# Attention and a routed expert layer: chosen experts only, side work between attention slots, scores on 64 contraction rows

## The reference

```
mask = where(diff > 0, -inf, 0);  cond = abs(diff) <= 64
mask = maximum(maximum(mask, where(cond, 0, -inf)), -1e9)   # all keys up to 64 ahead, and every key behind
attn = softmax(q * HEAD_DIM**-0.5 @ k.T + mask);  x = layernorm(x + (attn @ v) @ out_w.T + out_b)

scores = sigmoid(x @ router.T); sc = scores + e_bias
tidx   = top 4 of the 16 experts, out of the 2 best of 4 groups of 4;  tw = scores[tidx] / sum * 2.5
routed = sum over the 4 chosen e of tw[e] * (silu(x @ gate[e].T) * (x @ up[e].T)) @ down[e].T
shared = (silu(x @ sh_gate.T) * (x @ sh_up.T)) @ sh_down.T      # 2 experts' width, every token
x = layernorm(x + routed + shared)
```

## Time and profile before

| | us |
|---|---|
| median of 3 runs (range) | 1291.25 (1289.18 to 1295.77) |
| span of the profiled execution | 1287.9 |
| PE, DVE, ACT, POOL busy in it | 1214.8, 947.5, 625.9, 238.9 |
| projection, until the first attention slot | 0 to 99.8 |
| 16 attention rounds | 99.8 to about 644, some 31 to 34 each |
| expert stage | about 647 to 1283 |

### The profile page before, as it was taken

How to read it: one execution, slowest core, us unless ns; L and a number is a source line. 1 busy time by engine, 2 the same in 40 slices (tenths; PEclk the granted TensorE clock), 3 DMA queues, 4 the chain that set the end, 5 groups by cost and what they waited for, 6 DMA issues and landing times.

```text
span 1287.9 us, 28066 instructions
## 1 busy us (share of the span) xinstructions
PE 1214.8 (94%) x8448; PEld 644.6 (50%) x8448; DVE 947.5 (74%) x1975; ACT 625.9 (49%) x1366; POOL 238.9 (19%) x432
## 2 busy tenths in 40 slices
PE   7877999999999999999799999898998989989997
PEld 4543444444444444443356666565665656556564
DVE  7587888888888888887657776676776767757754
ACT  4415777777777777777633332323222232222332
POOL 8831222222222222222401010010200102000000
PEclk9998999999999999999999999898999999999999
DMA  5631111111111111110131232121312212122220
GB/s 166 187 116 53 38 39 39 37 37 37 37 37 37 37 34 32 34 36 14 46 84 61 48 99 59 61 71 43 90 49 63 77 51 90 50 47 77 59 82 33
DMA packets 62443, 76.78 MB, mean 60 GB/s; under 512 B 8992, under 2 KB 37408, under 8 KB 62368
## 3 DMA queue, kind: packets, MB, share of 16 engines
q1 hardware_dynamic: 60736, 72.80, 19.2%
q10 hardware_dynamic: 1632, 3.15, 0.8%
HBM read 62.94 MB, written 12.85 MB: 59 GB/s over the span
## 4 chain that ended last, share of the span: by engine, by line
PE 64%; DVE 13%; issue 9%; ACT 7%; SPq 2%; POOL 2%; DMA 2%; DVEq 0%; ACTq 0%; POOLq 0%
PE bank L759 16%; PE bank L604 11%; PE bank L572 9%; PE bank L587 9%; PE bank L772 9%; DVE hf L1192 3%; DVE sg L1185 3%; ACT hh L947 3%; ACT a_PT L863 3%; PE bank L647 2%; PE bank L575 2%; PE bank L688 1%; PE bank L628 1%; PE bank L651 1%; SPq L324 1%
## 5 line engine op out<-in xcount | busy, mean ns | idle before, releaser
L984 DVE TENSOR_REDUCE a_mx<-bank 128x1 f32<-128x512 f32 (+3 forms) x720 | 401.2, 618 | 73.7 <-PE bank L575 44.6
L863 ACT ACTIVATE a_PT<-bank 128x512 f32<-128x512 f32 (+4 forms) x832 | 357.0, 505 | 138.1 <-PE bank L587 137.5
L587 PE MATMUL bank<-a_QS,a_KS 113*128 113x512 f16 (+4 forms) x832 | 269.6, 331 | 11.4 <-ACT a_PT L863 6.1
L572 PE MATMUL bank<-a_KS,a_QS 112*128 112x512 f16 (+4 forms) x832 | 258.6, 332 | 15.5 <-DVE a_mx L984 8.3
L947 ACT CAST hh<-hf 128x512 f16<-128x512 f32 x144 | 89.0, 618 | 332.5 <-DVE hf L1192 332.5
L509 POOL TENSOR_SCALAR_AFFINE_SELECT a_PT<-a_PT 128x256 f32<-128x256 f32 (+1 forms) x288 | 109.6, 381 | 419.0 <-ACT a_PT L863 418.7
L604 PE MATMUL bank<-a_PT,a_VG 128*17 128x512 f32 (+4 forms) x1664 | 179.7, 504 | 6.4 <-POOL a_PT L509 6.4
L772 PE MATMUL bank<-dh,hh 128*128 128x256 f16 x576 | 159.0, 276 | 16.9 <-DVE z L1207 16.9
L1199 DVE TENSOR_TENSOR hl<-hf,hh 128x512 f16<-128x512 f32 x144 | 99.8, 693 | 99.4 <-ACT hh L947 99.4
L772 PE MATMUL bank<-dh,hl 128*128 128x256 f16 x576 | 159.1, 276 | 0.0
L772 PE MATMUL bank<-dl,hh 128*128 128x256 f16 x576 | 159.1, 276 | 0.0
(11 more groups left out here) (134 smaller groups left out, 1438.2 us busy)
## 6 DMA issues: line engine op xcount, KB each, us to landing
cb<-c_dram SPq DMA_DIRECT2D x128, 256.0 KB, 3.3
q_dram<-p_qk SPq DMA_DIRECT2D x32, 128.0 KB, 2.1
k_dram<-p_qk SPq DMA_DIRECT2D x32, 128.0 KB, 2.1
a_QS<-q_dram SPq DMA_DIRECT2D x64, 64.0 KB
a_KS<-k_dram SPq DMA_DIRECT2D x64, 64.0 KB
xb<-x SPq DMA_DIRECT2D x8, 512.0 KB, 3.6
out<-oo SPq DMA_DIRECT2D x8, 512.0 KB, 4.2
p_xf<-xT ACTq DMA_DIRECT2D x6, 512.0 KB, 4.2
```

Source lines behind the costliest of these rows:

```text
L572: mm = pe.matmul(bank[:, at:at + hi - lo], QS[p][0:MR, t // NT, h, t % NT * P:t % NT * P + P], KS[p][0:MR, piece, h % 2, 0:hi - lo], start ...
L587: pe.matmul(stbank[u % 3][:, 0:(qc + 1) * CH - q0], KS[p][0:MR + 1, kt // NT, h % 2, kt % NT * P:kt % NT * P + P], QS[p][0:MR + 1, qc, h, ...
L863: act.activation(PT[(p + i) % 2][:, h, 0:w], stbank[u % 3][:, 0:w], ACT.Exp)\
L984: dve.tensor_reduce(mx[:, piece, t // NT, heads[0]:heads[0] + n, t % NT], sbank[u % 3][:, 0:n * w].rearrange("p (h k) -> p h k", h=n), AX. ...
```

## The change

**Routed experts for chosen tokens only.** After the router, the four chosen experts of each token of a sequence (1024 tokens, 4096 pairs of token and expert) get slot numbers (`place`, in four parts on DVE, its largest operations 512 to 768 elements a partition, and `pos`, products with triangular ones on PE), so that the pairs of one expert lie together, each expert padded to whole blocks of 128. 48 blocks always hold them. POOL writes the token rows to their slots in DRAM by 32 indirect DMAs a sequence (`scatter`: 128 rows of 512 half-precision numbers each), SP reads two blocks at a time back transposed (`load_rows`, `dma_start_transpose`, 96 in all, three buffers), and PE computes them in a step "gu" of 24 matmuls of 128 columns with the weights at an address held in a register. ACT takes tanh in place of silu, DVE does two multiplications of 128x256, ACT and POOL make the high and low parts, PE does "y" (6 matmuls of 256), ACT copies it out (`y_out`, 128x512), SP stores it, and when all of a sequence is stored POOL fetches the rows of each token by 32 more indirect DMAs (`gather`), and DVE adds them up with their weights (`combine`, four operations of 128x256 for 128 tokens). The shared expert is done densely as before, in steps of 256 tokens. The broadcast loads from `c_dram` go, and so does L1185.

**Side work between attention slots.** The `Fori` loops go; `plan()` gives every side job a half-slot on each engine (`PE_AT`, `ACT_AT`, `DVE_AT`, `POOL_AT`, `SP_AT`; 416 half-slots are attention, 186 follow). The chunk steps (projection of the output, norms, router) of a sequence stand two to three half-slots apart after its four rounds, its experts in the rounds after. A side job is on its engine's one stream, with its own waits, between two pieces of attention. The last sequence's 28 pairs and shared steps, and what is left of the third, are behind attention. Counted by round, the steps "gu" are 0, 0, 0, 0, 2, 6, 4, 7, 3, 7, 9, 8, 3, 7, 7, 9, and 56 follow behind attention. Scores and transposed scores now share one ring of five banks (`take`), the side work has two.

**Scores on 64 rows.** Each head's rows start at 0 or 64 (`lane`), `KR = 48` rows are contracted, and the heads are taken in an order that changes between the two halves of the rows with each product. The mask product is split in the two halves as well: 64 of them in a round instead of 36; and 46 units instead of 45. DVE's two memsets of QS go and POOL's two of KS; DVE's memsets of KS rows become four, behind them stands a copy, and PE waits for that copy (`tri_done` 9) before its first projection product. v goes through DRAM, so POOL's copies of it go.

```diff
-MR = 112
...
+KR = 3 * HD
...
+def heads_of(slot):
+    units = share(slot)
+    first = UNITS[units[0][0]][4][0] if units else HG // 2
+    return (0, 2, 1, 3) if first >= HG // 2 else (2, 0, 3, 1)
+HEADS = [heads_of(i) for i in range(NSL)]
+def lane(h):
+    return 64 * (h // 2)
...
+        for t in range(BT):
+            for k in range(TOPK):
+                pool[q + 5 + (t * TOPK + k) * 2 // 3].append(("scatter", b, t, k))
...
+            q = put(("gu", b, n), h)
+            act[q + 1].append(("tanh", b, n))
+            dve[q + 2].append(("gate", b, n))
+            act[q + 3].append(("hh", b, n))
+            pool[q + 4].append(("hl", b, n))
+            if not shared:
+                sp[q - 5].append(("load_rows", b, n))
+                y = put(("y", b, n), q + 6)
+                act[y + 1].append(("y_out", b, n))
+                sp[y + 3].append(("store_y", b, n))
+            elif n % NSH:
+                y = put(("ysh", b, n), q + 6)
+                dve[y + 1].append(("add_shared", b, n))
...
+        at = y + 6
+        for t in range(BT):
+            for k in range(TOPK):
+                pool[at + (t * TOPK + k) * 2 // 3].append(("gather", b, t, k))
+            w = at + (t * TOPK + TOPK) * 2 // 3 + 3
+            dve[w].append(("combine", b, t))
...
+            def take(ring, *job):
+                at = RINGS[ring][turn[ring] % len(RINGS[ring])]
+                turn[ring] += 1
+                if at in holder:
+                    on.wait_ge(*emptied(holder[at]))
+                holder[at], bank_of[job] = job, at
+                return banks[at]
...
+                    r, c0, c1 = lane(h), m0 - P * t - WIN, m1 - P * t - WIN
+                    mm = pe.matmul(ps[:, at:at + hi - lo],
+                                   QS[p][r:r + KR, t // NT, h % 2, t % NT * P:t % NT * P + P],
+                                   KS[p][r:r + KR, piece, h % 2, 0:hi - lo], start=True, stop=(m1 <= m0))
+                    for part in range(2):
+                        f0 = max(c0, 64 * part)
+                        if c1 > f0:
+                            mm = pe.matmul(ps[:, at + f0 - c0 + m0 - lo:at + hi - lo], idb[r:r + 64, part, :],
+                                           tri[r:r + 64, part, f0:c1], start=False, stop=(part == 1 or c1 <= 64))
+                mm.then_inc(s["s_ready"], 1)
...
+                        i = routed_nth(b, n)
+                        u = 2 * (n - NPS)
+                        if u % REGS == 0:
+                            load_experts(b, u)
+                        on.wait_ge(xt_loaded[i % 3], i // 3 * 16 + 16)
+                        on.wait_ge(s["w_lo"], NX)
+                        cols = [(experts[b, u + v], v * P, P,
+                                 [(xt[i % 3][:, k, v * P:v * P + P], xt[i % 3][:, KD + k, v * P:v * P + P])
+                                  for k in range(KD)]) for v in range(2)]
+                    ps = take(ring, "gu", b, n)
+                    for e, at, v, tall in cols:
+                        for up in range(2):
+                            i = 0
+                            for lo, part in ((0, 0), (0, 1), (1, 0)):
+                                for k in range(KD):
+                                    mm = pe.matmul(ps[:, up * 2 * P + at:up * 2 * P + at + v],
+                                                   weights(e, (2 * up + lo) * D + k * P, P), tall[k][part],
+                                                   start=(i == 0), stop=(i == 5))
+                                    i += 1
+                    mm.then_inc(f["gu_ready"], 1)
...
+            pe.wait_ge(s["tri_done"], 9)
...
+                        on.wait_ge(f["scattered"], (b + 1) * BT * TOPK * 16)
+                        on.wait_ge(f["gu_ready"], nth(b, n) - 2)
+                        sp.dma_start_transpose(xt[i % 3][:], rows[b % 2][at:at + 2 * P, :])\
+                          .then_inc(xt_loaded[i % 3], 16)
...
+                    elif what == "scatter":
+                        b, t, k = a
+                        on.wait_ge(f["slot_done"], b + 1)
+                        on.wait_ge(f["row_lo"], b * NH2 + NH2)
+                        on.wait_ge(f["rows_zero"], 2 * NPR * 16)
+                        on.wait_ge(f["gu_ready"], nth(b - 1, 0) if b > 1 else 0)
+                        pool.indirect_dma_start(rows[b % 2], bass.IndirectOffsetOnAxis(ap=slot[b % 2][:, t, k:k + 1],
+                                                axis=0), XR[:, t, :], None).then_inc(f["scattered"], 16)
+                    elif what == "hl":
+                        q = nth(*a)
+                        on.wait_ge(f["hh_done"], q + 1)
+                        if q >= 4:
+                            on.wait_ge(*free_h(q - 4))
+                        pool.tensor_tensor(hl[q % 4][:], hf[q % 2][:], hh[q % 4][:], op=ALU.subtract)\
+                            .then_inc(f["hl_done"], 1)
+                    elif what == "gather":
+                        b, t, k = a
+                        i = b * BT + t
+                        for n in range(3):
+                            on.wait_ge(y_stored[n], (b + 1) * NPR // 3 * 16)
+                        on.wait_ge(f["comb_done"], i - 1)
+                        pool.indirect_dma_start(yg[i % 2][:, k, :], None, outs[b % 2], bass.IndirectOffsetOnAxis(
+                            ap=slot[b % 2][:, t, k:k + 1], axis=0)).then_inc(gathered[i % 2], 16)
...
-            dve.wait_ge(s["stack_zero"], 4)
             for a in KS:
-                dve.memset(a[96:P], 1.0).then_inc(s["stack_const"], 2)
-            def smax(G, p, u):
+                for r in (32, 96):
+                    dve.memset(a[r:r + 32], 1.0).then_inc(s["stack_const"], 1)
...
+                    elif what == "gate":
+                        q = nth(*a)
+                        ps = bank("gu", *a)
+                        on.wait_ge(f["tanh_done"], q + 1)
+                        dve.scalar_tensor_tensor(ga[q % 2][:], tq[q % 2][:], 1.0, ps[:, 0:2 * P], op0=ALU.add,
+                                                 op1=ALU.mult).then_inc(f["ga_done"], 1)
+                        on.wait_ge(f["ga_done"], q + 1)
+                        on.wait_ge(f["hl_done"], q - 1)
+                        dve.scalar_tensor_tensor(hf[q % 2][:], ps[:, 2 * P:4 * P], 0.5 / WSC / WSC, ga[q % 2][:],
+                                                 op0=ALU.mult, op1=ALU.mult).then_inc(f["h_done"], 1)
...
+                        for k in range(TOPK):
+                            ins = dve.scalar_tensor_tensor(zz, yg[i % 2][:, k, :], wk[b % 2][:, t, k:k + 1], zz,
+                                                           op0=ALU.mult, op1=ALU.add)
+                            ins.then_inc(f["comb_step"], 1)
+                            on.wait_ge(f["comb_step"], i * TOPK + k + 1)
...
-                if n >= NSH:
-                    e = n - NSH
-                    dve.wait_ge(c_loaded[e % NCB], (t * (NE // NCB) + e // NCB) * 16 + 16)
-                    dve.tensor_tensor(sg[n % 2][:], sg[n % 2][:], cb[e % NCB][:], op=ALU.mult)\
-                       .then_inc(f["sc_done"], 1)
-                    dve.wait_ge(f["sc_done"], t * NE + e + 1)
```

1665 lines of the change are left out of this document (924 added, 741 removed).

## The result

The changed kernel takes 1444.13 us (median of four executions, 1443.62 to 1453.54) beside 1292.88 for the kernel before: ratio 1.1196 with a 95% interval of 1.1156 to 1.1235, **12% slower**. The forecast was 1140, 12% faster, with a range to 1320. The profiled execution has a span of 1441.9 us; attention starts at 114.7 and ends at 1113.5, and 328.4 us follow.

The account below looks back on a forecast made before the run. PE was taken to bound the kernel nearly everywhere, with DVE next and fullest after the change. Start 110.5, attention 735, behind it 253, latencies 25 and unequal slots 15 made 1138.5 of span, forecast 1140 us, range 1010 to 1320.

Parts of the forecast that it names:

- rival without row overlap: Attention: products on the two row halves don't run at once, PE 31.7 us a round, whole 1195 us; chance 0.15.
- I take the gain: PE in attention: heads on different row halves run at once, both kinds of scores 8.7 us a round for 17.4.
- Took the fullest engine in each pair: Whole span: engine work summed over two slots, the fullest engine counted; 735 us in attention, 253 behind it.
- The forecast's own test: Attention rounds 1 to 3, without side work: 25 to 28 us expected, forecast wrong if over 30.
- Uneven rounds, 49 to 56 us for the heavy ones: Rounds 4, 5, 8, 9, 12, 13: routing and `place` give DVE 49 to 56 us.
- The part behind attention, 253 + 25: Behind attention: 253 us from maxima over four half-slots, gathers leading at the end, plus 25 of uncovered latencies.
- The indirect DMA at 1.04: Scatters and gathers on POOL: each taken at 1.04 us, the price of L525, as no row gave it.
- The register operations: Routed expert steps on PE: 20 register settings, 0.9 us, hidden beside matmuls; otherwise 2.4 us a step for 1.6.
- The wait at the start: Start: PE's first product waits for the copy behind four KS memsets, 10.4 us late; attention starts at about 110.
- POOL as the bound: Scatters and gathers: at 2.15 us each POOL leads, whole 1395 us, slower; chance 0.17.
- The row loads: Routed steps, a rival: transposed loads of 15 us latency pace them behind attention, whole 1250; part of others, 0.03.
- all four: The rivals: cheap indirect DMAs (1035 us, 0.20), no row overlap (1195, 0.15), dear POOL (1395, 0.17), latency-paced row loads (1250).

Follow-up runs that it names:

- all_behind: Changed kernel with scores on 112 rows and all side work from the output projection on placed behind attention; 1453.05 us, ratio 1.1272.
- rows112: Changed kernel with its third part undone: scores on 112 rows, one mask product, routed experts and side work kept; 1403.25 us, ratio 1.0861.
- short_max: Kernel before with scores for the maxima and the maxima over a quarter of the columns, no mask product; 1262.69 us, ratio 0.9774.
- route_once: Changed kernel with 112-row scores and the expert ranking on DVE left out for all chunks but the first two; 1351.21 us, ratio 1.0478.
- start_undone: Changed kernel with PE's wait for the copy of the mask moved behind the projection; 1444.07 us, ratio 1.1189.
- fill_scores: Changed kernel with two unused 128-row, 256-column products ahead of each product of transposed scores; 1556.39 us, ratio 1.2057.
- lanes_short_max: Changed kernel, 48 rows kept, with scores for the maxima and maxima over a quarter of the columns, no mask product; 1388.55 us, ratio 1.0717.
- same_lane: Changed kernel with heads ordered so successive score products stay on the same half of the rows as far as possible; 1474.91 us, ratio 1.1471.
- before_lanes: Kernel before with only the third part of the change, scores on 48 rows in alternating halves; 1374.26 us, ratio 1.0645.
- rows112_short_max: Changed kernel with 112-row scores, scores for the maxima and maxima over a quarter of the columns, no mask product; 1315.49 us, ratio 1.0174.

## Why the prediction was wrong

Differences of medians give the whole change step by step, from the kernel before at some 1290: routed experts and new code, all behind attention, +163 (all_behind); the side work moved into attention, -50 (rows112); scores on 48 rows, +41 (after). By the forecast's count the first part takes 284 us of work from PE (562 less 278). It cost 163: 110 in the stage, 15 at the start, and 38 in attention, whose rounds after the first take 35.5 to 37.7 us for 33.1.

The 303 us by which the span missed its sum can be laid out like this. The start is 4 of them. With full rows the forecast has attention at 791 + 15 (its rival without row overlap), and rows112 took 957: 151. The third part was to take 56 off that and put 42 on: 98. The part behind attention is the other 50.

**"I take the gain" (PE, attention alone): the halves can run at once, and the step failed twice over, 98 us.** A pair costs what one product does, as the 240.65 rows show. But the text took this for every product, 8.7 us for 17.4, and only 15 to 17 of 40 wide pairs ran together in rounds 1 to 3: in round 2 PE's weight loads wait 5.2 us for maxima and 5.1 us for exponentials, which is the likely reason. And all of the sum was at the full clock, since the kernel before had it, and nothing in the text asked whether it would stay with other products. It went to 0.82 on average in attention, for 0.91 with full rows. The Trainium skill (TensorEngine Tiling (Array Packing), Key Properties) says that a change of mode drains the array. The runs agree that a change costs something, by the estimate above 0.10 us between whole and half array. The 0.26 by which the text sized it is the fixed part of `weighted`, and too much for this. It wasn't the cause.

**"Took the fullest engine in each pair": the step that failed most, 151 us.** With PE at 22 us, DVE 25 and ACT 22, the maximum is 25, and with full rows it is PE's 31.7; rounds of the changed kernel with full rows and no side work take 36.1 us in the mean (578 for 16, all_behind), at full clock but for the first. Attention without side work was thus 578 us, for 507 by the forecast's own 31.7 and for the 400 to 450 that it took. Two mistakes are in it. The base was read from a stretch of 31.00 us that was a little less than a round; the round is 33.1 with 27.6 on DVE. And the maximum of sums holds only where engines can run ahead of each other, and the exchange of banks between PE and ACT seems not to allow that: short_max has 26.8, 13.6 and 23.6 us on the three engines and takes 31.0. The forecast's own test ("wrong if rounds 1 to 3 take over 30") caught it.

**Uneven rounds, 49 to 56 us for the heavy ones.** They took 72 to 86, and round 11, which isn't among them, 85. DVE had what was forecast (103 us in rounds 8 and 9 of rows112 together), but the ranking on it added to the rounds about what it took (route_once) and did not fill gaps. Over 16 rounds side work added 379 us in rows112 (957 - 578), where the forecast had about 284 with full rows (791 - 507). The clock has a part in this that no run takes out: with side work it is below 1.00 on full rows too.

**The part behind attention, 253 + 25.** 328 were measured. The gathers do end it, as forecast. Chain of waits at the end of the kernel after (start, us, what):

```profile
1426.60 0.95 POOL a_pool L964
1427.85 0.95 POOL a_pool L964
1429.10 2.71 DMA a_pool<-outs,e_slot
1431.84 0.50 DVE e_R L1378
```

One takes 0.95 us and the next starts 1.25 after it: the pitch, not the busy time, was the price. That is worth up to 17 us for the 82 gathers of this part (an estimate, 0.21 each). In addition, low parts (0.73 each) stand between them, and PE took 184 us for 138, at a granted clock of 0.75, with only 56% of that stretch busy. Without all indirect DMAs this part is still 268 us.

**Right.** The indirect DMA at 1.04 (0.97 to 1.00 measured). The Trainium skill (DMA: Bandwidth & Descriptors, Latency and other measured facts) puts the first byte of a DMA that POOL makes at about 1 us; POOL's busy time for one is of that size, and no row here shows a first byte. DVE's total (865 and 866). ACT leads nowhere. The register operations are hidden: 24 products with 20 of them take 1.34 us in the chain. The wait at the start does hold PE to 19.35, but of its 10.4 us attention gets 2.4, and the end nothing (start_undone).

**The rivals.** POOL as the bound ends on the side that came true, but by another cause: it decided from 1.67 us for one DMA, and the price was 1.25; without the DMAs the kernel is still at 1374. The row loads weren't late: a transposed load landed in 3.5 us, and no wait of L654 is put down to `xt`. "Row halves don't run at once" is refuted as a rule of the array, but was nearer to what the kernel did than the forecast: fewer than half of the pairs ran together. The time that came was in no rival, because all four shared the full clock and the maximum of sums. Slower had 0.17, and the head of the range, 1320, lay 124 us under the result.

**Left open.** What grants less clock to attention on 48 rows. These kernels show that it goes with the rows, not with the overlap (27 pairs in a round of fill_scores at 1.00, 5 in one of lanes_short_max at 0.50) and not with PE being less full alone (same_lane beside short_max); whether rows alone or the half-array setting too, no run separates. Nor does one divide the low clock of the rounds with side work between the rows and PE's waits. Why the bank ring settles at 31 to 38 us a round was seen as mutual waits and wasn't taken apart, nor was the 2.4 us between a round of all_behind (35.5) and one before (33.1). And the clock behind attention, 0.75, where all products are on whole rows but PE waits much, has been read only, as has the shorter expert stage of before_lanes.

## What to carry to other kernels

A change of a matmul's shape can change the clock it is granted: where the sum rests on a clock of 1.00, say so, and hold one case at the lower level. That two products can run at once isn't yet that they do: count how many reach the engine together. A maximum of engine sums is a floor; where two engines hand banks to and fro, take a whole period of the trace before, and ask which hand-over, not which sum, sets it. And side work in the one stream of an engine on that loop can cost its full time, though the engine is a third idle.

## What the runs showed of the hardware that was not expected

- Scores on 48 rows lower the granted clock: 44.50 us at 0.50 for 31.40 at 1.00 in the clearest pair of rounds, with as many products (lanes_short_max, rows112_short_max).
- Two products of 512 columns on different halves of the rows start together and cost as one, 0.22 us; going between half and whole array costs an estimated 0.10 us each time (fill_scores).
- An indirect DMA of 128 rows of 1 KB takes POOL 0.97 to 1.00 us, and 1.25 from one to the next.
